# Row tiles of the last expert layer: when the first expert's number is loaded, where the last shared sum is turned, and how the outputs are grouped

## The chip, the cores and the metric

The kernel runs on one core of a Trainium2 chip. The metric is the device time of one execution in microseconds. A core has five engines that run side by side and meet by semaphores: TensorE (PE, matrix products and turns of tiles, results go to PSUM banks), VectorE (DVE), ScalarE (ACT), GpSimd (POOL) and SyncE (SP, which issues transfers). Each executes its own list of instructions in order.

## The reference

Two layers over x, 8 x 256 tokens of 128 features. Each layer is a cross attention and a mixture of experts. The change lies in the last part of the second layer, which computes this:

```python
def _L1_ffn_ref(x_bsD, router_DE, w1_eDF, w3_eDF, w2_eFD, ws1_DF, ws3_DF, ws2_FD):
    B, S, D, E, F, K = (4, 128, 128, 8, 352, 1)
    scores_aE = x_aD @ router_DE
    vals_aK, idx_aK = jax.lax.top_k(scores_aE, K)
    ...
    gates_Ea = jax.nn.sigmoid(masked_aE).T
    routed_in_EaD = jax.lax.stop_gradient(gates_Ea[:, :, None] * x_aD[None, :, :])
    mid_EaF = jax.nn.silu(jnp.einsum('ead,edf->eaf', routed_in_EaD, w1_eDF)) * jnp.einsum('ead,edf->eaf', routed_in_EaD, w3_eDF)
    routed_out_EaD = jnp.einsum('eaf,efd->ead', mid_EaF, w2_eFD)
    shared_aD = jax.nn.silu(x_aD @ ws1_DF) * (x_aD @ ws3_DF) @ ws2_FD
    out_aD = shared_aD + routed_out_EaD.sum(axis=0)
```

Every token goes to one of 8 experts (gate and up matrices of 128 x 352, down matrix of 352 x 128) and to a shared expert of the same shape. The result is x plus both.

## The kernel before

**Shared expert.** The 2048 tokens are taken as 4 blocks of 512. The 352 inner features are cut in three (128, 128, 96), so there are 12 units (`shared_unit`, n = 0 to 11): six products for gate and up on PE, silu on ACT, a multiplication on DVE, and one unit later the down product (`shared_down`) that adds into the bank `SUM`. When a block's three units are done, ACT copies the sum (`copy_sum_1`), PE turns it in four pieces (`finish_1`, L728), and DVE adds it to x (`add_sum_1`, L1460). That sum is called `rest` below: it is what a token has beside its routed expert.

**Sorting.** DVE finds each token's expert and its place in a list that is sorted by expert and cut into tiles of 128 rows. There are 23 row tiles (`TILES`), each of one expert. POOL scatters the gated tokens to `rows_in` in device memory (16 scatters), and x with the shared sum to `rest_in` (16 scatters, `sort_rest`, L1941, four for each block, after that block's add). SP then reads both back in order of tiles, in groups of four tiles (`ROW_GROUPS`): `rows` after all scatters to `rows_in`, `rest_rows` (L2246) after all scatters to `rest_in`.

**Row tiles.** A loop on each engine runs over the tiles j:

- `rows_turn` (PE, L737) turns four tiles' rows at once, ACT and DVE split them into a high and a low part (`split_rows` L1088, `rest_of_rows` L1466). The first group is turned ahead of the loop, the others in the iterations j = 1, 5, 9, 13, 17.
- `gate_up` (PE, L358 to L360, six products) with the expert's matrices, whose address comes from a number: `value_load` (L745) fetches it from `expert_of` into a register of PE.
- `routed_silu` (ACT, L1093), `routed_mul` (DVE, L1473) give `mid`.
- `mid_turn` (PE, L760, three turns), one iteration later, into the bank `SIDE`. `copy_mid` brings the turned tile to SBUF in two parts, ACT (L1098), then DVE (L1489).
- `routed_down` (PE, L772, three products), two iterations later, into the bank `outs` or `misc` by the number of the output group.
- `add_rest` (DVE, L1484) adds `rest_rows` for a whole output group (`OUT_GROUPS`) when its last tile's down product is done. It stands on DVE behind the `routed_mul` and `copy_mid` of the same iteration.
- POOL then scatters the group's tiles to the output, one indirect transfer for each (L1954).

PE's list in iteration j is: products of tile j, turn of the next rows where due, turn of `mid` of tile j-1, down products of tile j-2. The order is written out by hand. A bank is written again only when its last reader is done (`bank_free`); `SIDE` is also the bank of `finish_1`, and `WEIGHT` that of `rows_turn`.

```python
OUT_GROUPS = [range(g, g + 2) for g in range(0, TILES - 3, 2)] + [range(g, g + 1) for g in range(TILES - 3, TILES)]
```

So the tiles go out in ten pairs (0 to 19) and three singles (20, 21, 22).

## Time and profile before

| | us |
|---|---|
| median of 3 runs | 693.57 (693.21 to 693.69) |
| the profiled execution | 696.93 |
| its span, first to last instruction | 695.5 |
| PE busy | 650.4 (94%) |
| DVE busy | 521.2 (75%) |
| POOL busy | 412.1 (59%) |
| ACT busy | 400.8 (58%) |
| row tiles: first product of tile 0 | 640.82 |
| last down product | 691.06 |
| last scatter issued | 693.26 |

The profile is of one execution on the chip; times in it are microseconds from the start of the span. A row of the timeline gives start, duration, engine, line, operation, tiles, count, and in brackets how long the engine had been idle before it and what ended that. "issue" there means that the engine waited for nothing that the profile shows. PE's ends are modelled: its instructions overlap, so the distance of two starts tells more than a duration. The granted clock of PE is at its full level through the row tiles.

### The profile page before, as it was taken

The page shows a single profiled execution, that of the slowest core. Times are in us where ns is not written, and L with a number is a line of the kernel's source. Part 1 is how long each engine was busy: PE and PEld are TensorE (multiplying, and loading weights), DVE is VectorE, ACT ScalarE, POOL GpSimd, SP SyncE. Part 2 cuts the span into 40 slices and gives each one's busy share as a digit, 9 for nine tenths or more (in the row PEclk, how much of TensorE's full clock was granted, in tenths as well). Part 3 has the DMA queues.
Part 4 walks back from the last instruction along what each step waited for, and adds up shares of the span by engine and source line. Part 5 has one row for each costly group of instructions (what it writes and reads, how often), then busy time and mean ns, then how long its engine had stood idle before and what let it go on. Part 6 is the DMA issues. An engine that isn't in the chain of part 4 may idle for free.

```text
span 695.5 us, 14219 instructions
## 1 busy us (share of the span) xinstructions
PE 650.4 (94%) x5301; PEld 343.9 (49%) x5301; DVE 521.2 (75%) x934; ACT 400.8 (58%) x568; POOL 412.1 (59%) x613
## 2 busy tenths in 40 slices
PE   5989999999999999999999999999999999988997
PEld 3333443434343666666656643334434344455897
DVE  4798999999888783942654568898998988766554
ACT  2057777777778634233222257777787777754443
POOL 3444558667412255769954565967977744547445
PEclk9999999999999999999999999999999999999999
DMA  6836635742600576485862406546645545104411
GB/s 175 217 98 163 164 107 126 180 125 60 156 2 3 119 187 139 147 175 144 195 149 78 94 23 149 161 129 153 175 142 120 153 109 177 35 31 133 121 33 39
DMA packets 66601, 84.97 MB, mean 122 GB/s; under 512 B 7776, under 2 KB 48624, under 8 KB 65024
## 3 DMA queue, kind: packets, MB, share of 16 engines
q1 hardware_dynamic: 63856, 79.44, 44.4%
q0 software_dynamic: 1760, 3.62, 1.6%
q10 hardware_dynamic: 916, 1.00, 0.6%
q8 instruction: 43, 0.70, 0.4%
q14 instruction: 26, 0.21, 0.1%
HBM read 57.57 MB, written 25.80 MB: 120 GB/s over the span
## 4 chain that ended last, share of the span: by engine, by line
PE 64%; ACT 12%; DVE 6%; POOL 5%; DMA 5%; issue 4%; SPq 3%; ACTq 0%; DVEq 0%; POOLq 0%
PE pair L497 11%; ACT prob L919 11%; PE misc L510 7%; PE outs L510 6%; PE outs L624 6%; PE pair L458 6%; PE pair L358 5%; PE pair L360 4%; PE pair L359 4%; PE misc L411 3%; DVE negmax L1206 2%; PE outs L396 2%; DMA col<-in_L_b 2%; DMA qstack<-mT 1%; POOL hid L1870 1%
## 5 line engine op out<-in xcount | busy, mean ns | idle before, releaser
L1206 DVE TENSOR_REDUCE negmax<-pair 128x2 f32<-128x1024 f32 x256 | 306.6, 1213 | 37.6 <-PE pair L458 31.6
L919 ACT ACTIVATE prob<-pair 128x1024 f32<-128x1024 f32 x256 | 260.2, 1025 | 89.7 <-PE pair L497 85.3
L497 PE MATMUL pair<-qstack,kstack 54*128 54x256 bf16 x1024 | 100.4, 274 | 20.8 <-ACT prob L919 19.3
L458 PE MATMUL pair<-kstack,qstack 51*128 51x512 bf16 (+1 forms) x512 | 98.1, 379 | 1.6 <-DVE negmax L1206 0.8
L1440 DVE TENSOR_TENSOR hid<-pair,silu 128x512 f32<-128x512 f32 x68 | 46.7, 688 | 70.1 <-PE pair L360 51.3
L497 PEld LDWEIGHTS pair<-qstack,kstack 54*128 54x128 bf16 x1024 | 29.9, 94 | 126.0 <-ACT prob L919 101.1
L1066 ACT ACTIVATE silu<-pair 128x512 f32<-128x512 f32 x68 | 40.6, 599 | 88.6 <-PE pair L360 86.5
L510 PE MATMUL outs<-prob,vaug 128*32 128x256 f32 x1024 | 83.4, 390 | 0.0
L510 PE MATMUL misc<-prob,vaug 128*32 128x256 f32 x1024 | 81.0, 391 | 0.3
L624 PE MATMUL outs<-hid,down 128*128 128x512 f32 x136 | 70.3, 598 | 1.7 <-POOL hid L1870 1.6
L358 PE MATMUL pair<-xT,eh 128*128 128x512 f32 x136 | 70.3, 517 | 0.0
L1870 POOL TENSOR_TENSOR hid<-hid,w_here 128x512 f32<-128x512 f32 x32 | 41.0, 1282 | 40.5 <-DVE hid L1440 40.5
L1792 POOL CAST mparts<-negmax 128x16 bf16<-128x16 f32 x32 | 6.5, 202 | 92.6 <-DVE negmax L1206 92.6
L1870 POOL TENSOR_TENSOR hid<-hid,w_there 128x512 f32<-128x512 f32 x32 | 41.1, 1288 | 26.6 <-DVE hid L1440 26.6
L360 PE MATMUL pair<-xT,e_lo 128*128 128x512 f32 x136 | 53.7, 395 | 0.0
L359 PE MATMUL pair<-xT,eh 128*128 128x512 f32 x136 | 53.2, 391 | 0.0
L1684 POOL TENSOR_SCALAR xn<-x,mv,rstd 128x128 f32<-128x128 f32 x48 | 37.9, 797 | 2.5
L1954 POOL DMA_INDIRECT out_x<-rows,token_of x23 | 22.0, 957 | 25.2 <-DVE rows L1484 20.9
L458 PEld LDWEIGHTS pair<-kstack,qstack 51*128 51x128 bf16 (+1 forms) x512 | 25.3, 94 | 21.9 <-issue 14.6
L1715 POOL TENSOR_TENSOR work<-work,rope 128x512 f32<-128x512 f32 (+1 forms) x32 | 31.4, 1001 | 5.1 <-DMA work<-work 5.0
L358 PEld LDWEIGHTS pair<-xT,eh 128*128 128x128 f32 x136 | 25.6, 188 | 15.2 <-issue 11.7
L510 PEld LDWEIGHTS misc<-prob,vaug 128*32 128x32 f32 x1024 | 20.6, 108 | 24.4 <-issue 11.8
(290 smaller groups left out, 1086.4 us busy)
## 6 DMA issues: line engine op xcount, KB each, us to landing
kstack<-k_terms SPq DMA_DIRECT2D x30, 384.0 KB
w_here<-w_rows SPq DMA_DIRECT2D x32, 256.0 KB, 4.8
w_there<-w_rows SPq DMA_DIRECT2D x32, 256.0 KB, 5.1
k_terms<-kparts SPq DMA_DIRECT2D x16, 384.0 KB, 2.6
qstack<-q_terms SPq DMA_DIRECT2D x30, 192.0 KB, 4.3
ctx_nat<-in_ctxT SPq DMA_DIRECT2D x16, 256.0 KB, 3.2
k_terms<-kparts SPq DMA_DIRECT2D x16, 256.0 KB, 2.9
w_nat<-in_L_gu SPq DMA_DIRECT2D x9, 352.0 KB, 3.7
```

The costliest lines, as they stand in the source:

```text
L358: nc.tensor.matmul(to, w[0], v[0], start=True, stop=False)
L359: nc.tensor.matmul(to, w[0], v[1], start=False, stop=False)
L360: return nc.tensor.matmul(to, w[1], v[0], start=False, stop=True)
L458: return nc.tensor.matmul(to, qstack[n % 3][rows, g, qt * P:(qt + 1) * P], kstack[n % 3][rows, g, :], start=True, stop=True)
L497: e = nc.tensor.matmul(bank[m + r][:, k * SQ:(k + 1) * SQ], kstack[n % 3][rows, g, (c + k) * P:(c + k + 1) * P], qstack[n % 3][rows, g, :] ...
L510: e = nc.tensor.matmul(bank[m][32 * j:32 * j + 32, (quad % 2) * SQ:(quad % 2 + 1) * SQ], vaug[:, KC * (n % 3) + c, h * VC:h * VC + 32], pr ...
L624: nc.tensor.matmul(bank[SUM], down0[:, u, :], hid0[:, m % 4, :], start=place == 0, stop=place == EP).then_inc(d_done, 1)
L919: nc.scalar.activation(prob[:, quad % 2, 2 * g:2 * g + 2, c:c + 2, :].rearrange("p j c q -> p j (c q)"), pair[t_pair(n, step)][:, :, :], A ...
L1066: nc.scalar.activation(silu0[:, m % 2, :], bank[m % 2], ACT.Silu).then_inc(silu_done, 1)
L1206: nc.vector.tensor_reduce(negmax[:, n % 2, 2 * g:2 * g + 2, qt], pair[score_pair(n, step)][:, :, :], AX.X, ALU.max, negate=True).then_inc( ...
L1440: nc.vector.tensor_tensor(hid0[:, m % 4, :], bank[2 + m % 2], silu0[:, m % 2, :], ALU.mult).then_inc(u_mul, 1)
L1870: nc.gpsimd.tensor_tensor(hid0[:, m % 4, :], hid0[:, m % 4, :], weight_buffer(g)[:, w % GROUP, :], ALU.mult).then_inc(w_mul, 1)
```

## The change

Three edits.

1. The number of the first expert is loaded by PE ahead of the first `rows_turn`, not at the head of tile 0.
2. The last block's shared sum (`finish_1(NB - 1)`) is turned behind tile 0's products, not ahead of them. The waits for the weights' low parts stay ahead of tile 0.
3. The output groups are two of four tiles (0 to 3, 4 to 7), five pairs (8 to 17) and five singles (18 to 22). The last tile's `mid` is turned in the bank `WEIGHT`, which no `rows_turn` uses any more then; the two copies read it from there.

```diff
-OUT_GROUPS = [range(g, g + 2) for g in range(0, TILES - 3, 2)] + [range(g, g + 1) for g in range(TILES - 3, TILES)]
+OUT_GROUPS = [range(0, 4), range(4, 8)] + [range(g, g + 2) for g in range(8, TILES - 5, 2)] + [range(g, g + 1) for g in range(TILES - 5, TILES)]
...
+def turning(j):
+
+    return WEIGHT if j == TILES - 1 else SIDE
...
+            def load_expert(j):
+                expert[j] = nc.tensor.value_load(expert_of[0:1, j:j + 1], min_val=0, max_val=E1 - 1)
+
             def gate_up(j):
                 i, k, m = j // 4, j % 4, j % 2
-                expert[j] = e = nc.tensor.value_load(expert_of[0:1, j:j + 1], min_val=0, max_val=E1 - 1)
+                if j > 0:
+                    load_expert(j)
+                e = expert[j]
...
             def mid_turn(j):
                 pe.wait_ge(mid_set, j + 1)
-                bank_free(SIDE)
+                m = turning(j)
+                bank_free(m)
                 for c, (f0, fn) in enumerate(FC):
-                    e = nc.tensor.transpose(bank[SIDE][0:fn, c * P:(c + 1) * P], mid[:, j % 2, f0:f0 + fn], ident[:, :])
+                    e = nc.tensor.transpose(bank[m][0:fn, c * P:(c + 1) * P], mid[:, j % 2, f0:f0 + fn], ident[:, :])
                 e.then_inc(mid_turned, 1)
-                left[SIDE] = midT_b, j + 1
+                left[m] = midT_b, j + 1
...
+                pe.wait_ge(experts_known, 1)
+                load_expert(0)
                 rows_turn(0)
                 shared_down(NB * len(FC) - 1)
-                finish_1(NB - 1)
                 pe.wait_ge(w_low, EP + 1 + len(GU_EARLY))
                 pe.wait_ge(gu_lo, len(GU_LATE))
-                pe.wait_ge(experts_known, 1)
                 for j in range(TILES + 2):
                     if j < TILES:
                         gate_up(j)
+                    if j == 0:
+                        finish_1(NB - 1)
```

The two `copy_mid` (ACT and DVE) read `bank[turning(j)]` instead of `bank[SIDE]`.

PE, from the last unit's down product to tile 0, before. `TENSOR_LOAD expert_of` is the number's load, L728 the turns of the shared sum, L737 those of the rows:

```order
L720 MATMUL outs<-hid,down 128x512 [waits su_mul]
L737 MATMUL pair<-ident,rows 128x128 [waits ld_rows0]
L737 MATMUL pair<-ident,rows 128x128 x3
L720 MATMUL outs<-hid,down 128x512 [waits su_mul]
L728 MATMUL pair<-ident,yT 128x128 [waits ssum_added,ssum_copied]
L728 MATMUL pair<-ident,yT 128x128 x3
L745 TENSOR_LOAD expert_of [waits experts_known,gu_lo,w_low]
L745 ISA x2
L358 ISA [waits ssilu_done,gxT_lo]
L358 MATMUL pair<-gu,gxT 128x352
```

PE, the same place in the changed kernel. The lines are numbered anew: L725 is the down product, L749 the load, L742 the rows, L363 to L365 the products, L733 the shared sum:

```order
L725 MATMUL outs<-hid,down 128x512 [waits su_mul]
L749 TENSOR_LOAD expert_of [waits experts_known]
L749 ISA x2
L742 MATMUL pair<-ident,rows 128x128 [waits ld_rows0]
L742 MATMUL pair<-ident,rows 128x128 x3
L725 MATMUL outs<-hid,down 128x512 [waits su_mul]
L363 ISA [waits gxT_lo,ssilu_done,gu_lo,w_low]
L363 MATMUL pair<-gu,gxT 128x352
...
L365 MATMUL pair<-gu,gxT 128x352
L733 MATMUL pair<-ident,yT 128x128 [waits ssum_added,ssum_copied]
L733 MATMUL pair<-ident,yT 128x128 x3
```

The load has moved from between the shared sum and tile 0 to ahead of the rows; the shared sum's turns have moved from ahead of tile 0's six products to behind them.

DVE, the first add of `rest_rows`, before. It stands ahead of tile 4's multiplication (the first L1473 below it), and holds two tiles (128x2x128):

```order
L1489 COPY hid<-pair 96x128 [waits midT_a]
L1484 TENSOR_TENSOR rows<-outs,rest_rows 128x2x128 [waits rd_done,ld_rest0]
L1473 TENSOR_TENSOR mid<-pair,silu 128x352 [waits mid_turned,rsilu_done,ru_done]
L1489 COPY hid<-pair 96x128 [waits midT_a]
L1473 TENSOR_TENSOR mid<-pair,silu 128x352 [waits mid_turned,rsilu_done,ru_done]
L1466 TENSOR_TENSOR gxT<-pair,gxT 128x512 [waits gxT_hi]
```

DVE in the changed kernel, from tile 4's multiplication on (L1486 is the multiplication, L1479 the split of the rows, L1502 the copy, L1497 the add):

```order
L1486 TENSOR_TENSOR mid<-pair,silu 128x352 [waits mid_turned,rsilu_done,ru_done]
L1502 COPY hid<-pair 96x128 [waits midT_a]
L1486 TENSOR_TENSOR mid<-pair,silu 128x352 [waits mid_turned,rsilu_done,ru_done]
L1479 TENSOR_TENSOR gxT<-pair,gxT 128x512 [waits gxT_hi]
L1480 CAST token_of<-rows 128x4
L1502 COPY hid<-pair 96x128 [waits midT_a]
L1497 TENSOR_TENSOR rows<-outs,rest_rows 128x4x128 [waits rd_done,ld_rest0]
L1486 TENSOR_TENSOR mid<-pair,silu 128x352 [waits mid_turned,rsilu_done,ru_done]
```

The first add has moved behind the multiplications of tiles 4 and 5 and behind the split of the third group of rows, and is of four tiles. On DVE and POOL the end of the list differs by the same table: the adds of tiles 18 and 19 are single there.

## Rows read from the trace of the kernel before

**Rows 1.** The page's first part: busy us, share and count of each engine.

```profile
PE 650.4 (94%) x5301; PEld 343.9 (49%) x5301; DVE 521.2 (75%) x934; ACT 400.8 (58%) x568; POOL 412.1 (59%) x613
```

**Rows 2.** Busy by stretch: length, then PE, PEld, DVE, ACT, POOL, clock, DMA.

```profile
652.00:655.00 3.00, 2.23 (x16) 1.91 (x15) 2.56 (x8) 1.08 (x3) 1.97 (x3) 1.00 1.02 298
...
664.70:689.00 24.30, 24.30 (x185) 23.88 (x186) 12.83 (x34) 10.87 (x26) 11.48 (x13) 1.00 0.11 34
```

**Rows 3.** Timeline of PE from the first rows' turn to tile 1's turn.

```profile
637.45 0.60 PE L737 MATMUL pair<-ident,rows 128*128 128x128 f32 x4
...
639.60 0.66 PE L728 MATMUL pair<-ident,yT 128*128 128x128 f32 x4 [0.69 <-ACT yT L1081]
640.82 0.42 PE L358 MATMUL pair<-gu,gxT 128*128 x1 [0.56 <-issue]
...
642.01 0.42 PE L358 MATMUL pair<-gu,gxT 128*128 x1
...
643.07 0.60 PE L737 MATMUL pair<-ident,rows 128*128 128x128 f32 x4
643.51 0.49 PE L760 MATMUL pair<-ident,mid 128*128 128x128 f32 x3
643.75 0.41 PE L358 MATMUL pair<-gu,gxT 128*128 x1
...
645.44 0.52 PE L760 MATMUL pair<-ident,mid 128*128 128x128 f32 x3 [0.48 <-DVE hid L1489]
```

**Rows 4.** Timeline of DVE at the same place.

```profile
638.72 0.69 DVE L1466 TENSOR_TENSOR gxT<-pair,gxT 128x512 fp32r<-128x512 f32 x1 [1.19 <-ACT gxT L1088]
...
642.16 0.53 DVE L1473 TENSOR_TENSOR mid<-pair,silu 128x352 f32<-128x352 f32 x1 [1.17 <-ACT silu L1093]
```

**Rows 5.** Timeline of DVE, two of the adds of `rest_rows`.

```profile
651.72 0.43 DVE L1484 TENSOR_TENSOR rows<-outs,rest_rows 128x256 f32<-128x256 f32 x1 [2.85 <-DMA rest_rows<-rest_in]
...
663.23 0.41 DVE L1484 TENSOR_TENSOR rows<-misc,rest_rows 128x256 f32<-128x256 f32 x1
```

**Rows 6.** Timeline of PE: tiles 5, 7, 8, 9, 11, and tile 4's turn.

```profile
650.52 0.41 PE L358 MATMUL pair<-gu,gxT 128*128 x1
...
652.91 0.52 PE L760 MATMUL pair<-ident,mid 128*128 128x128 f32 x3 [0.75 <-DVE hid L1489]
...
656.11 0.41 PE L358 MATMUL pair<-gu,gxT 128*128 x1
...
658.07 0.41 PE L358 MATMUL pair<-gu,gxT 128*128 x1
...
660.03 0.41 PE L358 MATMUL pair<-gu,gxT 128*128 x1
...
664.64 0.42 PE L358 MATMUL pair<-gu,gxT 128*128 x1
```

**Rows 7.** Timeline of the end, POOL, DVE and PE.

```profile
688.21 0.96 POOL L1954 DMA_INDIRECT out_x<-rows,token_of  x1 [1.71 <-DVE rows L1484]
...
689.23 0.29 DVE L1489 COPY hid<-pair 96x128 f32<-96x128 f32 x1 [0.15 <-ACT hid L1098]
...
689.48 0.29 DVE L1484 TENSOR_TENSOR rows<-outs,rest_rows 128x128 f32<-128x128 f32 x1
689.66 0.52 PE L760 MATMUL pair<-ident,mid 128*128 128x128 f32 x3 [0.22 <-DVE hid L1489]
...
693.26 0.96 POOL L1954 DMA_INDIRECT out_x<-rows,token_of  x1 [0.30 <-issue]
```

**Rows 8.** DMA issues of the output: count, median us from issue to landing.

```profile
out_x<-rows,token_of POOLq DMA_INDIRECT x23, 2.2
```

**Rows 9.** Timeline of POOL: the first scatter of `rest_in`'s last block.

```profile
642.27 0.96 POOL L1941 DMA_INDIRECT rest_in<-x,row_of  x1 [0.30 <-issue]
```

**Rows 10.** The chain that ended last: the last `rest_in` scatter, the first `rest_rows` transfer.

```profile
646.06 2.23 DMA rest_in<-x,row_of
...
648.30 3.39 DMA rest_rows<-rest_in
```

More of the change, by code:

```diff
@@ L1097, in copy_mid @@
                 act.wait_ge(rd_done, j - 1)
-                nc.scalar.activation(hid1[:, j % 2, 0:2 * P], bank[SIDE][:, 0:2 * P], ACT.Copy).then_inc(midT_a, 1)
+                nc.scalar.activation(hid1[:, j % 2, 0:2 * P], bank[turning(j)][:, 0:2 * P], ACT.Copy).then_inc(midT_a, 1)
             def ffn_1():
@@ L1488, in copy_mid @@
                 ve.wait_ge(midT_a, j + 1)
-                nc.vector.tensor_copy(hid1[0:FC[2][1], j % 2, 2 * P:3 * P], bank[SIDE][0:FC[2][1], 2 * P:3 * P]).then_inc(midT_b, 1)
+                nc.vector.tensor_copy(hid1[0:FC[2][1], j % 2, 2 * P:3 * P], bank[turning(j)][0:FC[2][1], 2 * P:3 * P]).then_inc(midT_b, 1)
             tiles_first, first, end_first, full_first, base, tiles, new, begin, end, shift = (plan[:, i, :] for i in range(10))
```

## The prediction

> **What bounds the kernel now.** I first read the share of each engine: TensorE (PE) is busy 94% of the span, all others below 76% [rows 1]. That share says little about this change, which touches only the last 60 us, so I went on to the busy time by stretch. In the long middle of the row tiles (664.7 to 689.0 us) PE is busy in every microsecond: 24.30 of 24.30 [rows 2]. There a tile costs what its PE work costs, and nothing in the change alters that. What can move is where PE is not full: the step from the shared expert into the first tiles, the place around 652 to 655 us, where PE is busy 2.23 of 3.00 us [rows 2], and what follows PE's last product.
>
> I read these three places in the timeline, engine by engine. "Tile j" is row tile 0 to 22. For each tile PE runs six gate and up products, three turns of `mid` and the down products; in the PE rows the first L358 of a tile is its start.
>
> At the start, PE turns the first rows (637.45), runs the last shared down product, waits for ACT's copy of the sum, turns that at 639.60, and starts tile 0 at 640.82 after 0.56 us in which it waited for nothing that the profile shows [rows 3]. The rows that tile 0 needs were split by DVE at 638.72 + 0.69 = 639.41 [rows 4]. So tile 0 comes 1.41 us after its data.
>
> In the middle, DVE stood still for 2.85 us until 651.72, for the first transfer of `rest_rows` [rows 5]. It was already in the add of tiles 0 and 1, and the multiplications of tiles 4 and 5 were queued behind it. PE waited 0.75 us for that [rows 6].
>
> At the end the chain leaves PE. POOL sends one scatter per tile, 0.96 us plus 0.30 of issue. It sits idle for 1.71 us, starts tile 18 at 688.21 and then runs five back to back until the start of the last at 693.26 [rows 7]. A scatter lands 2.2 us after its issue [rows 8], and that of the last one is the end of the span.
>
> **Part 1: the front.** Two edits. The number of tile 0 is loaded before the rows are turned, and the four turns of the last shared sum go behind tile 0's six products. Cost of a number load on PE: from the sum's turns to tile 0 is 640.82 - 639.60 = 1.22 us; four turns take PE 0.44 us (as at 643.07, after which the next work starts at 643.51) [rows 3]. That leaves 0.78 us for the load and its waits. From tile 0 to tile 1, 1.19 us pass for products that need some 0.97, so there part of the load is hidden. I take 0.7 us.
>
> After the change tile 0 waits only for 639.41. PE starts 0.14 us after a DVE instruction that it waits for (DVE ends at 689.23 + 0.29 = 689.52, PE starts at 689.66 [rows 7]), and a few waits stand before it; I take 639.75. Then tile 0 takes its 1.19 us, as now with tile 1's load in it, and the four turns of the sum add 0.41 to 0.44. Tile 1 starts at about 641.35 instead of 642.01: **0.66 us earlier**. The gain is half of the 1.07 us by which tile 0 moves, because the turns used to lie in front of it and now lie behind.
>
> Does it survive? The turned sum is now ready at about 640.8 + 0.66 = 641.46, so DVE adds it until 642.15, and tile 0's multiplication, queued behind that add, starts at 642.15, where it starts today (642.16 [rows 4]). So tile 0 itself gains nothing. But the next thing that holds PE is the turn of tile 1 at 645.44, behind the second group of rows (turned at 643.07, their split, then DVE's copy) [rows 3]. That chain hangs on the turn of the rows, which comes 0.66 us earlier (2.37 us from 643.07 to 645.44 stay). It gives 644.8, and PE, with tile 2 starting near 643.7 as now, is ready at 644.7. So the 0.66 holds from tile 1's turn on.
>
> The load that stands before the first rows' turn: PE has products in front of it there without a gap, and a load that stands behind a full stretch of products costs nothing between the later tiles (PE is busy throughout [rows 2]). I take 0, since that row is the nearest. Bounds: 0 and 0.78.
>
> The moved turns also feed POOL: the scatters of the last block of `rest_in` wait for this add. They start at 642.27 today, right behind four others [rows 9]. With the add ending at 642.15 they start at about 642.45. Some 0.2 us late, and it must be carried to the next part.
>
> **Part 2: outputs in fours.** The add of tiles 0 to 3 now stands on DVE behind tile 5's multiplication and the third split of rows, not behind tile 3's multiplication. Today's landing is at 648.30 + 3.39 = 651.69 [rows 10]; with the 0.2 it is 651.9. When does DVE get there? Tiles 9 to 11 have the same shape of work without a wait: tile 9 starts at 660.03, the add at 663.23, so 3.20 us later [rows 5, 6]. Tile 5 would start at 650.52 - 0.66 = 649.86, the add at 653.06. That is 1.2 us after the landing: no wait. The stretch from tile 5 to tile 7 takes 656.11 - 650.52 = 5.59 us now, that from 9 to 11 takes 664.64 - 660.03 = 4.61 us [rows 6]. The difference, **0.98 us**, is what the standstill costs PE. An add of four tiles takes 0.69 instead of 0.41 to 0.43 us (0.69 is what the split of 512 columns takes [rows 4], the pairs' adds stand in [rows 5]). The multiplication behind it is 0.1 to 0.3 us later, and PE needs it some 1.3 us after that: covered. The same holds for the add of tiles 4 to 7. POOL gets four scatters at once, 5.0 us of work (4 x 1.26) per 7.8 us of tiles (4 x 1.96, the distance of tile 8 to tile 9 [rows 6]), and has caught up long before the end.
>
> **Part 3: the end.** Tiles 18 and 19 are sent singly. POOL is idle from 686.50, and tile 18's sum is done by then (it comes one tile, some 1.96 us, before tile 19's), so its scatter leaves there and no longer pushes the rest. In today's clock: tile 19 at 688.1; tile 20's add ends at 689.48 + 0.29 = 689.77, its scatter starts at 690.05; then 691.31 and 692.57. Today it is 693.26: **0.69 us**. The last tile's turn goes to another bank, so it need not wait for DVE's copy (PE idle 0.22 by the profile's ends [rows 7]). Worth 0.2 to 0.4 us on PE; it brings the last sum to about 692.2 and so leaves POOL as the bound. Without it the data would be there at 692.6, so that edit alone is worth under 0.1.
>
> **The sum.** 0.66 + 0.98 + 0.69 = 2.33 us. The profiled span of 695.5 us becomes 693.2. The profiled run took 696.93 us, 1.4 more than its span, and 3.4 more than the median of the unprofiled runs (693.57). I take the difference over: 693.57 - 2.33 = **691.24 us**.
>
> **The rivals.**
> *The front gives nothing (20%).* Either the load before the first rows' turn is not hidden (then everything behind is 0.7 later and eats the 0.66), or the 0.56 us was not the load. Result 691.24 + 0.66 = 691.9. For it: no row shows a number load before a turn. Against: the loads between the later tiles cost nothing.
> By the Trainium skill, "Perfetto Trace Analysis", section "Tensor Engine Instruction (MATMUL, LD_WEIGHTS)", a product that waits for a semaphore waits in a queue of the engine while the sequencer goes on to the next instruction. By that rule the load had already run under the wait for the sum, and moving it would bring nothing: 691.9. The trace speaks against it: after the wait, tile 0 still comes 0.78 us later than its four turns allow [rows 3].
>
> *The wait for `rest_rows` stays in some form (12%).* If the transfer lands later than 654.1, four tiles' add holds tile 6's multiplication past PE's need. Then Part 2 gives nothing and the result is 692.2. For it: one group of four now hangs on one wait, and the chain of scatters before it starts 0.2 later. Against: 2.2 us of room.
>
> *Slower (4%).* The same mechanism from a certain point: the last block's scatters to `rest_in` wait for the sum that is now turned later. Each microsecond by which that add is late past 642.15 moves the landing by one. PE stalls from a landing at 654.1 on; the gains are gone at 656.4, and at 657.8, 6.1 us later than today, the kernel is 0.2% slower (695.0). The rows show 0.2 us of that.
>
> *Only the end gains (5%).* 692.9, if both PE gains are met by other waits.
>
> **Numbers.** The forecast has 59%. Differences under 0.2% (1.4 us) can't be told from none here, so "faster" means below 692.2. Faster: nearly all of the first case, most of the second, a third of the third: 0.78. Same 0.18, slower 0.04. Range: below, if PE's tile 0 gains all of its 1.07 us and the rest goes a little better, 690.4; above, the third case, 692.3.
>
> **What would show it.** Right: tile 0 starts near 639.75 and tile 1 near 641.35; DVE's first `rest_rows` add is 128x512, near 653, with no DMA wait; tile 7 at about 654.5 (now 656.11); the last scatter starts near 690.9 in the new span, with short idle times between POOL's last five. Wrong: a gap before the first rows' turn; a DMA wait on DVE; tile 2's turn as late as now; a last scatter that waits for nothing while its data is long there.

## The result

| | before | after |
|---|---|---|
| median of 20 runs, us | 694.75 (691.93 to 697.15) | 693.39 (690.45 to 694.73) |
| ratio, 95% interval | | 0.9972 (0.9960 to 0.9985) |
| profiled execution, its span | 696.93, 695.5 | 693.53, 692.2 |
| measured again, beside 23 runs of before | 695.35 | 692.34 (12 runs), ratio 0.9966 (0.9950 to 0.9982) |

By these ratios the change makes the kernel faster by 1.95 us (1.0 to 2.8), and by 2.36 us in the second comparison. The plain differences of the medians are 1.36 and 3.01 us. The forecast was 2.33 us. The time itself, 693.39, lies 1.1 us above the end of the stated range. On two other chips (whole and whole5 below), on which the kernel before takes 709 to 710 us, the same comparison shows no gain: 0.9991 (0.9968 to 1.0014) and 1.0007 (0.9983 to 1.0031). The experiments come back to them.

Even the executions near 695 us differ by up to 1.8 us in when they reach the row tiles, with the same code up to there but for the number load. I therefore count from the start of the first rows' turn (before 637.45, after 636.56). The profile after, PE's timeline at the start (columns: start, us, engine, line, operation; in brackets the idle time before it and what ended it):

```profile
636.56 0.60 PE L742 MATMUL pair<-ident,rows 128*128 128x128 f32 x4
...
638.87 0.43 PE L363 MATMUL pair<-gu,gxT 128*128 x1 [0.85 <-DVE gxT L1479]
...
639.95 0.60 PE L733 MATMUL pair<-ident,yT 128*128 128x128 f32 x4
640.30 0.41 PE L363 MATMUL pair<-gu,gxT 128*128 x1
...
643.71 0.52 PE L771 MATMUL pair<-ident,mid 128*128 128x128 f32 x3
```

Tile 0 starts 2.31 us after the rows' turn (3.37 in [rows 3]) and now waits for its data, DVE's split. Tile 1 comes at 3.74 instead of 4.56, the turn of its `mid` at 7.15 instead of 7.99.

The same stretch on DVE, and its first `rest_rows` add:

```profile
637.83 0.69 DVE L1479 TENSOR_TENSOR gxT<-pair,gxT 128x512 fp32r<-128x512 f32 x1 [1.19 <-ACT gxT L1101]
...
640.58 0.69 DVE L1473 TENSOR_TENSOR x<-pair,x 128x512 f32<-128x512 f32 x1 [1.99 <-PE pair L733]
...
652.08 0.68 DVE L1497 TENSOR_TENSOR rows<-outs,rest_rows 128x512 f32<-128x512 f32 x1
```

The wait of 2.85 us [rows 5] is gone; the add now takes four tiles at once. PE, tiles 5, 7, 9 and 11 in turn:

```profile
648.89 0.41 PE L363 MATMUL pair<-gu,gxT 128*128 x1
...
653.44 0.42 PE L363 MATMUL pair<-gu,gxT 128*128 x1
...
657.37 0.41 PE L363 MATMUL pair<-gu,gxT 128*128 x1
...
661.98 0.43 PE L363 MATMUL pair<-gu,gxT 128*128 x1
```

Tile 5 to tile 7 takes 4.55 us (5.59 in [rows 6]), about the same as tile 9 to 11 (4.61). By stretch (length, then busy us of PE, PEld, DVE, ACT, POOL, granted clock, DMA share, GB/s) the hole that stood there is filled, and the long stretch stays full:

```profile
652.00:655.00 3.00, 3.00 (x24) 2.81 (x23) 1.70 (x5) 1.31 (x3) 1.67 (x2) 1.00 1.01 291
664.70:689.00 24.30, 24.20 (x185) 23.27 (x183) 12.85 (x35) 10.58 (x25) 14.00 (x16) 1.00 0.13 41
```

The end, on POOL and DVE:

```profile
685.47 0.95 POOL L1967 DMA_INDIRECT out_x<-rows,token_of  x1 [0.31 <-DVE rows L1497]
687.44 0.96 POOL L1967 DMA_INDIRECT out_x<-rows,token_of  x1 [1.02 <-DVE rows L1497]
688.70 0.96 POOL L1967 DMA_INDIRECT out_x<-rows,token_of  x1 [0.30 <-issue]
689.96 0.95 POOL L1967 DMA_INDIRECT out_x<-rows,token_of  x1 [0.30 <-issue]
...
689.01 0.29 DVE L1497 TENSOR_TENSOR rows<-misc,rest_rows 128x128 f32<-128x128 f32 x1 [0.71 <-PE misc L783]
```

The backlog of five scatters [rows 7] has shrunk to three, and the last starts 0.66 us after its data.

### The profile page after: what moved, and what is told of

It is laid out like the page before. It is cut to its first block, busy times and chain, and to the rows that moved or that the text cites. A ratio compares the mean times of both kernels' runs of the same rounds, so it can differ in the third digit from the quotient of the medians.

```text
span 692.2 us, 14218 instructions
## 1 busy us (share of the span) xinstructions
PE 650.1 (94%) x5301; PEld 344.3 (50%) x5301; DVE 521.0 (75%) x933; ACT 400.4 (58%) x568; POOL 412.0 (60%) x613
## 4 chain that ended last, share of the span: by engine, by line
PE 69%; ACT 12%; DVE 6%; DMA 4%; POOL 3%; issue 3%; SPq 2%; ACTq 0%; DVEq 0%; POOLq 0%
PE pair L502 11%; ACT prob L932 11%; PE misc L515 7%; PE outs L629 7%; PE outs L515 6%; PE pair L363 6%; PE pair L463 6%; PE pair L365 5%; PE pair L364 5%; PE misc L416 3%; DVE negmax L1219 2%; PE outs L401 2%; DMA col<-in_L_b 2%; DMA qstack<-mT 1%; PE outs L725 1%
## 5 line engine op out<-in xcount | busy, mean ns | idle before, releaser
L363 PE MATMUL pair<-xT,eh 128*128 128x512 f32 x136 | 70.3, 517 | 0.0
L365 PE MATMUL pair<-xT,e_lo 128*128 128x512 f32 x136 | 53.7, 395 | 0.0
L363 PEld LDWEIGHTS pair<-xT,eh 128*128 128x128 f32 x136 | 25.6, 188 | 15.1 <-issue 11.7
```

The source lines that it names most:

```text
L363: nc.tensor.matmul(to, w[0], v[0], start=True, stop=False)
L365: return nc.tensor.matmul(to, w[1], v[0], start=False, stop=True)
```

## Experiments

Marks of the runs, in us behind each kernel's first rows' turn ("front" is the number load ahead and the sum's turn behind the first products):

| kernel | tile 0 | tile 1 | tile 5 | tile 7 | tile 22 | last scatter |
|---|---|---|---|---|---|---|
| before | 3.37 | 4.56 | 13.07 | 18.66 | 49.78 | 55.81 |
| after | 2.31 | 3.74 | 12.33 | 16.88 | 48.06 | 53.40 |
| whole6 (after again) | 2.31 | 3.74 | 12.37 | 16.92 | 48.12 | 53.45 |
| e_nofours | 2.31 | 3.74 | 12.39 | 20.64 | 51.80 | 57.15 |
| e_front2 | 2.31 | 3.72 | 16.54 | 21.37 | 53.03 | 59.26 |
| e_front3 | 2.36 | 4.04 | 17.64 | 22.19 | 53.71 | 59.89 |
| whole5 (after again) | 2.38 | 4.07 | 16.47 | 21.02 | 57.84 | 63.54 |
| e_fours4 | 4.54 | 5.73 | 19.59 | 24.18 | 59.36 | 65.55 |
| e_end2 | 4.39 | 6.31 | 19.69 | 24.42 | 55.99 | 61.68 |

The first four rows are from chips on which the kernel before takes about 695 us, the others from chips on which it takes 708 to 710. What differs there is told below; up to some 590 us both kinds of run agree to within 5 us. The kernel before was timed there but not traced; e_end2, which differs from it only at the end of the list, stands in for it. A *stop* below is a time in which an engine stands still although the profile shows its inputs there.

### First set: each part of the front, and the fours

**e_front**: front alone (`turning(j)` is always `SIDE`, `OUT_GROUPS` as before).

> The two edits at the front alone (number of tile 0 loaded ahead of the first rows' turn, last shared sum turned behind tile 0); output groups and the last turn as before. All times here are counted from the start of the first rows' turn on PE, since the stages ahead differ by some tenths of a us from run to run. Before: tile 0 at 3.37, tile 1 at 4.56, tile 7 at 18.66, last scatter at 55.81. Whole change: 2.31, 3.74, 16.88, 53.40. Theory (parts add up): tile 0 at 2.3, tile 1 at 3.7 (0.8 earlier than before). DVE still stands still at the first add of rest_rows, and since the landing of that transfer doesn't move (or moves 0.2 later), PE's gain of 0.8 is lost in a longer wait there: tile 7 at 18.7 to 18.9, last scatter at 55.8 to 56.0, no gain at all. Rival (the sum as I forecast it, each part on its own): tile 7 at 17.9 and the last scatter at 55.0.

704.83 us, a single time, beside 708.14 of before. Tile 0 comes at 3.12 and not at 2.3, because the rows' split on ACT and DVE is late in this run. As in before, DVE's first add waits for the transfer:

```profile
658.07 0.43 DVE L1497 TENSOR_TENSOR rows<-outs,rest_rows 128x256 f32<-128x256 f32 x1 [2.58 <-DMA rest_rows<-rest_in]
```

**e_load**: the number load ahead, the sum's turn where it was.

```diff
+                pe.wait_ge(experts_known, 1)
+                load_expert(0)
                 rows_turn(0)
```

> Only the number of tile 0 is loaded ahead; the last shared sum is turned ahead of tile 0, as before. Counted from the first rows' turn (before: shared sum's turns at 2.15, tile 0 at 3.37). Theory: the 1.22 us from the shared sum's turns to tile 0 shrink to the 0.44 that four turns take and some tenths for waits, tile 0 at 2.6 to 2.8; the first rows' turn comes no later behind the down product ahead of it (0.85 us after it, as before). Rival (a waiting product doesn't hold up the load behind it, the 0.56 us were something else): tile 0 stays at 3.3 to 3.4. Rival (load not hidden): rows' turn 0.7 later behind the down product.

PE from the rows' turn to tile 0:

```profile
642.26 0.60 PE L742 MATMUL pair<-ident,rows 128*128 128x128 f32 x4
...
645.43 0.66 PE L733 MATMUL pair<-ident,yT 128*128 128x128 f32 x4 [0.69 <-ACT yT L1093]
645.84 0.41 PE L363 MATMUL pair<-gu,gxT 128*128 x1
```

From the sum's turn to tile 0 it is 0.41 us; in [rows 3] it is 1.22, and in the six other traced kernels that keep the load there (e_fours to e_fours4, e_end, e_end2) it is 1.19 to 1.29. So the number load cost PE 0.81 us, although it stands behind an instruction that waited 0.69 us for ACT. The time of the whole run (707.52) says nothing here: tile 3 comes 7.8 us after tile 2 (2.4 in the changed kernel).

**e_sumbehind**: the turn behind, the load where it was (in `gate_up`).

```diff
-                finish_1(NB - 1)
                 pe.wait_ge(experts_known, 1)
 ...
                     gate_up(j)
+                    if j == 0:
+                        finish_1(NB - 1)
```

> Only the last shared sum is turned behind tile 0; the number of tile 0 is loaded at its head, as before. Counted from the first rows' turn. Theory: the number load has the time until the rows' split at 1.96 (the last down product and the wait for the split) to run in, so tile 0 comes at 2.3, as in the whole change, and tile 1 at 3.7: then the load ahead brings nothing once the sum is out of the way. Rival: the load stands behind the wait for the last down product's input and is exposed, tile 0 at 2.9 to 3.0.

707.91 us. Tile 0 at 2.58, tile 1 at 4.00. PE around it:

```profile
646.44 1.12 PE L725 MATMUL outs<-hid,down 96*128 96x512 f32 x2 [0.80 <-DVE hid L1466]
647.62 0.43 PE L363 MATMUL pair<-gu,gxT 128*128 x1
```

The last shared down product waited 0.80 us for a late multiplication on DVE, and tile 0 follows it directly. So the 0.27 us by which tile 0 is later than in the changed kernel is no price of the load. The turn behind alone brings at least 0.79 of tile 0's 1.06 us, and the load alone took 0.81 from the same stretch: the two edits are not a sum. Whether the load ahead still brings something once the turn is out of the way is not shown.

**e_fours**: `OUT_GROUPS` with two groups of four, three singles, nothing else.

> Only the first two output groups are of four tiles; front and end as before. Counted from the first rows' turn (before: tile 5 at 13.07, tile 7 at 18.66, last scatter at 55.81). Theory: DVE's first add of rest_rows waits for no transfer, or for under 0.3 us, tile 5 to tile 7 takes 4.6 instead of 5.6, tile 7 at 17.7, last scatter at 54.8 (1.0 earlier). Rival (the wait for rest_rows only moves to the add of four): tile 7 stays at 18.4 to 18.7.

716.67 us, a single time, with stops of many microseconds in the row tiles. Inconclusive; e_fours2 to e_fours4 repeat it.

### Second set: the parts with intervals

**whole** is the changed kernel, **e_front2** and **e_fours2** repeat the above, **e_end** has five singles at the end and pairs before:

```diff
-OUT_GROUPS = [range(g, g + 2) for g in range(0, TILES - 3, 2)] + [range(g, g + 1) for g in range(TILES - 3, TILES)]
+OUT_GROUPS = [range(g, g + 2) for g in range(0, TILES - 5, 2)] + [range(g, g + 1) for g in range(TILES - 5, TILES)]
```

> The whole change once more, as the yardstick of this set. Theory: 1.4 to 2.8 us faster than the kernel before on the same chip (2.0 by the comparison so far). In the profile, counted from the first rows' turn on PE (before: tile 0 at 3.37, tile 1 at 4.56, tile 7 at 18.66, last scatter at 55.81): 2.31, 3.74, 16.88, 53.40, to within 0.3. Rival (the differences of single runs are as large as the change, and the profile of the first comparison was a lucky one): other intervals by over 0.5, with engines idle for something that isn't in the program.

> The two edits at the front alone, once more (in the first run of it engines stood still for microseconds while all their inputs were there, so that its intervals can't be read). Theory: tile 0 at 2.3, tile 1 at 3.7 after the first rows' turn, but the first add of rest_rows waits longer for its transfer (3.5 us instead of 2.85) and tile 7 stays at 18.7 to 18.9, last scatter at 55.8 to 56.0: no gain, 0 to 0.2 us slower. Rival (as I summed it up): tile 7 at 17.9, last scatter at 55.0, 0.7 faster.

> The two groups of four alone, once more. Theory: tile 5 to tile 7 takes 4.6 instead of 5.6, tile 7 at 17.7, last scatter at 54.8, 1.0 us faster than before. Rival (the wait for rest_rows only moves to the add of four): tile 7 at 18.4 to 18.7.

> Only the end: tiles 18 and 19 single, last tile turned in the other bank; the first groups are pairs and the front is as before. Theory: tile 7 at 18.7 as before, last scatter 0.65 to 0.7 earlier, at 55.1; 0.7 us faster. Rival (PE, not POOL, bounds the end once tiles 18 and 19 are single): the last scatter waits for the last add, 55.3 to 55.5.

| | us | ratio, 95% |
|---|---|---|
| whole | 709.43 | 0.9991 (0.9968 to 1.0014) |
| e_front2 | 708.18 | 0.9961 (0.9940 to 0.9981) |
| e_fours2 | 712.70 | 1.0034 (1.0010 to 1.0057) |
| e_end | 710.25 | 0.9992 (0.9974 to 1.0011) |

Against the expectations, the front alone was the best and the fours alone lost.

The traces show one half of the reason: on these chips the wait that the fours remove is mostly not there. Stops in tiles 1 to 5 bring DVE to its first `rest_rows` add after the transfer has landed. With pairs that add waited for the transfer in e_front alone (2.58 us); in e_load, e_sumbehind, e_front2, e_front3, e_end and e_end2 it stood idle for 0.03 to 0.65 us, and not for the transfer. Tile 5 to tile 7 takes 4.55 to 4.85 us in these six, against 4.55 to 4.63 in whole, whole5 and e_fours2 to e_fours4. So there was little for the fours to gain, and no wait for the transfer that could take the front's gain back. What the fours lost is told with the fourth set.

From tile 22 to the last scatter e_end takes 5.76 us (6.23 in e_front2, whose end is that of before), about the gain that was expected for it.

### Third set: the price of a load, a late landing, another place for the add

**e_loads3** leaves two more loads of the same number beside the first (useless work). **e_late4** delays the last block of `rest_in` by four additions on POOL (useless work too). **e_next** moves the last shared sum to behind tile 1's products and the turn of tile 0's `mid` (into the bank `misc`) and the adds of the fours one iteration later.

```diff
 load_expert(0)
+load_expert(0)
+load_expert(0)
```
```diff
+for i in range(4 if blk == NB - 1 else 0):
+    nc.gpsimd.tensor_tensor(wnat[:, :, :], wnat[:, :, :], wnat[:, :, :], ALU.add).then_inc(filled, 1)
+    pool.wait_ge(filled, i + 1)
```
```diff
-                    if j == 0:
+                    if j == 1:
                         finish_1(NB - 1)
...
+                        if j == g[-1] + (3 if len(g) == 4 else 2):
+                            add_rest(i)
```

> The whole change, but the number of tile 0 is loaded three times ahead of the first rows' turn (the first two loads have no use). In the whole change the first rows' turn starts 0.86 us after the first pass of the down product ahead of it, 0.85 without the load: one load there costs nothing. Theory (PE's instructions run ahead of its products there, by more than one load): with two more loads the turn comes 0.7 to 1.6 us later, since two more can't all be hidden, and tile 0 still 2.3 after the turn. Rival (the loads never hold up products): 0.86 stays. Each load's price can be read from it. Where the chip holds engines up by itself (they stand still with all inputs there, at the same places in all kernels of a chip), only distances without such a stop are compared.

> The whole change, with four additions on GpSimd (384 columns each, of no use) ahead of the last block's scatters to rest_in; about 1.3 us each, so the landing of rest_rows is some 5 us later. Theory: from a landing 2.2 us later than in the whole change on, PE pays each further microsecond: tile 5 to tile 7 takes 4.55 + 2.5 to 3 us, DVE waits 3.5 to 4 us for the transfer at the add of four tiles, and the kernel is 0.3 to 1 us slower than before. Rival (PE has more room, since tile 6's multiplication is all that hangs on it): tile 5 to 7 stays under 5.5.

> The whole change, and the last shared sum goes further back: turned behind tile 0's turn into the bank misc, which nobody uses then, and added on DVE behind the second split of rows; in return the adds of four tiles stand one tile later on DVE. Theory: the second rows' turn comes 0.4 earlier, at 4.4 instead of 4.8 after the first, and since the chain to tile 1's turn hangs on it, tiles 3 and later are 0.2 to 0.4 earlier than in the whole change; the transfer of rest_rows lands 2.7 later, which the later add just covers (no stop at tile 7). 0.3 us faster than the whole change, which the timing can't tell. Rival (the later landing comes back as a wait): tile 7 and later as in the whole change or later, with a DMA wait on DVE.

> The two groups of four alone, a third time. In the second run they were 0.34% slower than before on their chip, on which engines stopped for microseconds with all their inputs there, at the same places in every kernel. Theory (on a chip without these stops the effect is the one I summed up): tile 5 to tile 7 4.6 instead of 5.6, 1.0 us faster. Rival (the groups of four themselves cost, e.g. by the scatters that go out late and at once): 0.2 to 0.5% slower again, and the profile shows it behind tile 7, where POOL's scatters or DVE hold PE.

e_loads3, 714.79 us, one run, PE:

```profile
648.09 1.02 PE L725 MATMUL outs<-hid,down 128*128 128x512 f32 x2
649.30 0.65 PE L742 MATMUL pair<-ident,rows 128*128 128x128 f32 x4 [0.20 <-issue]
```

The rows' turn comes 1.21 us behind the down product; after it is 0.86 (636.56 behind 635.70), and 0.85 before. So one load is hidden there and of three 0.35 us shows, in one run; I had expected 0.7 to 1.6 us more.

e_late4, 704.83 us, one run: POOL and DVE:

```profile
646.73 3.55 POOL L1965 TENSOR_TENSOR wnat<-wnat 128x384 f32<-128x384 f32 x4
...
654.36 0.96 POOL L1956 DMA_INDIRECT rest_in<-x,row_of  x1 [0.30 <-issue]
```
```profile
659.64 0.69 DVE L1499 TENSOR_TENSOR rows<-outs,rest_rows 128x512 f32<-128x512 f32 x1 [1.19 <-DMA rest_rows<-rest_in]
```

With the block 3.8 us later the group of four does wait, for 1.19 us, so the room is finite. The price that I expected (a wait of 3.5 to 4 us, 2.5 to 3 us more from tile 5 to tile 7) did not come. That stretch takes 5.42 us instead of 4.55, which is the rival's figure, and its extra time lies ahead of the add, where ACT stood still for 2.10 us; tile 6 to tile 7, behind the add, takes 1.99. When PE begins to pay for a late landing is not shown. e_next gained nothing (710.89 us, ratio 1.0013, 0.9993 to 1.0033), and e_fours3 lost again (710.85 us, 1.0033, 1.0013 to 1.0053).

### Fourth set: the parts once more

> The whole change again, on another chip. By the theory that the three parts gain what the two undisturbed profiles show (0.84 us at tile 1's turn, about 0.9 more by tile 7, 0.63 at the end, 2.41 in all), the ratio is 0.9965 where engines do not stop with their inputs there; first tile 2.3 us and last scatter some 53.4 us behind the first rows' turn. By the rival that the gain of the two long profiles was one of level between runs, the ratio is 1.000. Where stops of microseconds lie in the row tiles again, the ratio is unclear and the marks up to the first stop are what counts.

> The kernel before with its first eight output tiles in two groups of four, nothing else. By the theory that the grouping takes away the wait of rest_rows' first add (2.85 us) without a price, it is 0.7 to 1.1 us faster than before (ratio 0.9985 to 0.999) where engines do not stop. By the rival that the grouping has a price of its own, which the two runs on stopping chips (1.0034 and 1.0033) showed, it is slower by some 2.3 us again, and the rows of tiles 0 to 8 show where.

> The kernel before with its last five output tiles scattered one by one instead of three. Theory: last scatter 0.6 us earlier (ratio 0.999); last add's data ready 0.3 us ahead of the last scatter's start. Rival: the two added scatters cost their 1.26 us apart each and nothing is gained, 1.000 to 1.002.

> The kernel before with the first expert's number loaded ahead and the last shared sum's turn behind the first gate products. Theory: tile 0 at 2.3 and tile 1's turn at 7.1 us behind the first rows' turn (before 3.37 and 7.99), of which 0 to 0.8 us reach the end, since the wait of the first rest_rows add (2.85 us before) takes the rest back: that add waits longer by what the tiles are earlier, ratio 0.999 to 1.000. Rival: nothing takes it back and the ratio is that of the 10 runs earlier, 0.996 (2.8 us).

| | us | ratio, 95% |
|---|---|---|
| whole5 | 709.71 | 1.0007 (0.9983 to 1.0031) |
| e_fours4 | 712.69 | 1.0059 (1.0027 to 1.0090) |
| e_end2 | 709.78 | 1.0006 (0.9991 to 1.0021) |
| e_front3 | 707.14 | 0.9972 (0.9945 to 0.9999) |

The same order again, again on a chip with stops. In e_fours4 one of them stands at tile 13. A scatter on POOL and the copy on ACT there:

```profile
682.39 0.96 POOL L1954 DMA_INDIRECT out_x<-rows,token_of  x1 [0.30 <-issue]
684.63 0.39 ACT L1098 ACTIVATE hid<-pair 128x256 f32<-128x256 f32 x1 [2.37 <-remote]
```

Tile 9 to 10 takes 3.26 us and tile 13 to 14 5.80 in it; in the traced kernels whose first groups are pairs both take 2.40 to 2.42. From tile 9 to tile 16 the seven kernels with pairs take 15.2 to 15.6 us on these chips (15.1 in the trace of before, which has no stops). Eight kernels with the fours take 16.7 to 20.6 us, and e_next 23.0. So every kernel with the fours has stops there, of 1 to 8 us in all, that the pairs don't have.

They go with something that the rows do show. In each of these nine kernels POOL sends four scatters back to back and then four or six more (in e_fours4 at 667.29 to 672.05 and at 676.07 to 683.35), and in each a stop begins inside or at the end of such a run. The pairs send at most two at a time there. In e_next, whose adds of four stand an iteration later, the stops begin at tiles 10 and 14 and not 9 and 13. That is where they lie, not a cause: on the chips without stops the changed kernel sends the same four and six back to back, and nothing stops. What makes engines stop is not shown.

### Fifth set: the change without its fours

```diff
-OUT_GROUPS = [range(0, 4), range(4, 8)] + [range(g, g + 2) for g in range(8, TILES - 5, 2)] + ...
+OUT_GROUPS = [range(g, g + 2) for g in range(0, TILES - 5, 2)] + ...
```

> The changed kernel with its first eight tiles back in groups of two: front and end of the change without the fours. Theory for a chip on which engines stop with their inputs there: the grouping in fours costs what extra stops take around tiles 9 to 15 (each kernel that has it showed intervals of 3.3 to 6.4 us there, none without it did), so this one keeps the front's gain: ratio 0.996 to 0.997 (2 to 3 us) and even intervals of tiles 9 to 15. Rival: the fours gain their 0.9 us and the others' sum is what it is on an undisturbed chip: ratio 0.998, worse than the whole change. On a chip without such stops both theories give 0.9978 to 0.9985 for it and the DMA wait of the first rest_rows add grows to 3.6 us.

> The whole change beside the one without fours, on the same chip. By the theory of a place-dependent price of the fours: ratio 0.999 to 1.001 on a stopping chip, 2 us behind the kernel without them. By the rival: 0.9965 to 0.9975, 0.9 us ahead of it. On a chip without stops: 0.9965 and ahead of it by the wait that the fours take away.

This set ran on a chip without stops. e_nofours took 696.36 us, ratio 1.0013 (0.9992 to 1.0033); whole6 692.34 us, ratio 0.9966 (0.9965 expected). My figure for such a chip, 0.9978 to 0.9985, was wrong: without the fours the other two parts together show no gain. The wait of the first add, expected at 3.6 us, was 4.05. DVE and PE of e_nofours at tiles 4 to 6:

```profile
650.42 0.43 DVE L1497 TENSOR_TENSOR rows<-outs,rest_rows 128x256 f32<-128x256 f32 x1 [4.05 <-DMA rest_rows<-rest_in]
```
```profile
651.61 0.52 PE L771 MATMUL pair<-ident,mid 128*128 128x128 f32 x3 [1.95 <-DVE hid L1502]
```

The front brings DVE to the add earlier, the transfer does not land earlier, so the wait grows from 2.85 to 4.05 us and PE's idle time from 0.75 [rows 6] to 1.95. Then comes something that before did not have. By stretch, e_nofours (the column after POOL's is the granted clock):

```profile
651.00:652.00 1.00, 0.39 (x4) 0.42 (x5) 1.00 (x4) 0.00 (x0) 0.88 (x1) 1.00 1.08 321
652.00:653.00 1.00, 1.00 (x9) 0.87 (x8) 1.00 (x4) 0.38 (x1) 0.69 (x2) 0.82 1.10 310
653.00:654.00 1.00, 1.00 (x4) 1.00 (x5) 0.28 (x1) 0.00 (x0) 0.69 (x2) 0.50 0.62 189
654.00:655.00 1.00, 1.00 (x5) 0.93 (x5) 0.09 (x1) 0.46 (x1) 0.69 (x2) 0.50 0.08 25
655.00:656.00 1.00, 1.00 (x7) 0.99 (x6) 0.47 (x2) 0.38 (x1) 0.87 (x1) 0.50 0.20 66
656.00:657.00 1.00, 1.00 (x9) 1.00 (x9) 0.25 (x1) 0.00 (x0) 0.00 (x0) 0.97 0.20 66
```

After the idle time TensorE ran for more than 3 us at a granted clock of 0.50, which is 1.2 of its 2.4 GHz: 4 to 5 products in a microsecond instead of 9 to 10. Tile 6 to 7 took 3.51 us instead of 1.99. From tile 5 to 7 that makes 8.25 us, 3.70 more than with the fours (4.55). DVE in whole6, for comparison, has no such wait:

```profile
651.93 0.68 DVE L1497 TENSOR_TENSOR rows<-outs,rest_rows 128x512 f32<-128x512 f32 x1
```

The clock also orders the single runs. Of e_nofours' 12, four have a mean clock of 0.997 or more, with a median of 693.89 us; the other eight 697.61. Of before's 23 beside them, 12 have it (694.66), 11 don't (695.68). In whole6 it is 8 (692.07) and 4 (693.20).

So the loss is not in every execution. In the four at the higher clock the kernel without its fours is 0.77 us faster than before at that clock, about what the end alone gives (0.69): there the longer wait takes back the front and no more. In the eight others the clock costs on top. That is a reading of four and eight runs, and only one of them was traced.

## Why the prediction was right in its steps and missed in its time

**The front, 0.66: right, 0.82 measured.** Tile 0 comes 1.06 us earlier, as forecast (1.07). For tile 0 to tile 1 with the turns between them I had 1.60 us, and it took 1.43: the turns take 0.35 there, and tile 0's products up to them 1.08 instead of 1.19, so tile 1's load seems better hidden. From tile 1's turn on 0.84 remains, as the "does it survive" step had it. The load ahead of the rows' turn costs nothing (0.86 against 0.85); e_loads3 shows where that ends. The rival that the front gives nothing falls for the whole change, on the chips without stops. In the Trainium skill, "Perfetto Trace Analysis", section "Tensor Engine Instruction (MATMUL, LD_WEIGHTS)", the sequencer goes on while a product waits. By that rule the load in the kernel before would have been hidden already; the trace of e_load does not agree, since tile 0 moved by 0.81 us against the sum's turn.

**The middle, 0.98: right, 1.04 measured (5.59 to 4.55).** The last block's first scatter came 4.99 us behind the rows' turn; forecast 5.00. DVE reached the add at 15.52; forecast 15.61. What I had as a fixed number is the room. I put the landing at 14.45 and the room at 1.2 us. With the last block's scatters at the same marks, the transfer was issued and landed at 11.03 and 14.77 in e_nofours, at 12.34 and 15.04 in after and at 11.01 and 14.08 in whole6. DVE's add came 0.48 us behind the landing in after and 1.49 in whole6. It was enough in both, in after by little. Why the transfer was issued 1.3 us later there is not shown.

What the step did not say is how much hangs on it. It priced the fours against the kernel before. Beside the front they are worth 3.76 us at tile 7 in the traced executions (20.64 without them, 16.88 with them). From tile 5 to tile 7 that is 1.04 for the old wait, 1.20 by which the front makes PE's idle time longer (1.95 for 0.75), and some 1.5 for the clock (3.51 us for 1.99 from tile 6 to 7), which not every execution pays.

So the three terms do not add up part by part, and the sum came out right only because all three were in it: 0.66 + 0.69 without 0.98 would have been 1.35 faster, and measured is no gain (1.0013). The same error stands in the rival whose "wait for `rest_rows` stays": it was priced at 692.2, with the front's 0.66 kept.

**The end, 0.69: right.** From tile 22's start to the last scatter it is 6.03 us before and 5.34 after (48.06 to 53.40), 0.69 less. On the chips with stops it is 6.18 (e_front3) and 5.69 (e_end2), 0.49 less. The end alone was not run on a chip without stops; where it was, its ratios (0.9992 and 1.0006) can't be told from 1. The last scatter now starts 0.66 us after its data; I had 0.37 (692.2 to 692.57). POOL is the bound at the end, as forecast, with 0.3 us more room than I gave it.

**The sum.** Tile 7 comes 1.78 us earlier (forecast 1.64), the last scatter 2.41 (forecast 2.33). The three parts measured add up to 2.55; some 0.1 us is lost again between tiles 1 and 5 and between tiles 7 and 22. That it lands within 0.1 of the forecast is in part luck. The ratios say 1.95 and 2.36 us.

**The failed step is the last line of the sum**: "693.57 - 2.33". It took the median of three runs that lay within 0.5 us of each other as the level to subtract from. Twenty runs of the same kernel spread from 691.93 to 697.15, with a median of 694.75, 1.18 above the three. The median after lies 2.15 us above the forecast, 1.18 of it by the level and 0.97 because the medians differ by 1.36 and not by 2.33. My range had room for the second and none for the first: without the level's 1.18, 693.39 would have been 692.2, just inside. Part of the spread is the clock: of the 20 runs after, the six with a mean clock of 0.999 or 1.000 have a median of 691.71 us, the eight at 0.994 to 0.996 one of 694.11. The row that warned of it was there: the profiled execution took 3.4 us more than the median of the three, and I carried that difference over as if it belonged to profiling.

**What stays open** is why the fours lose on chips with stops. The rows put the loss into stops at tiles 9 to 16, inside or behind runs of four to six scatters, but don't tell what causes them. The kernel without fours was to test it there and ran on a chip without stops. Nor were the front alone, the fours alone or the end alone run on a chip without stops: what each would give there alone is read from the traces of the kernels that have them together.

## What to carry to other kernels

Price a wait at the length that it has after the other parts of the same change: work that is shortened ahead of a late transfer only lengthens the wait, and can cost TensorE its clock on top, so move the consumer of the transfer first. Three runs that agree say little of where twenty will lie: forecast the difference, and give the range the spread of the level. Time a part on the kind of chip on which the whole was timed; a wait that one chip has can be missing on another.

## What the runs showed of the hardware

- A number load into a register of PE cost it 0.81 us where products wait on it (e_load), even though the instruction ahead of it waits 0.69 us for another engine. Ahead of the first rows' turn, behind a filled stretch, one cost nothing (0.86 against 0.85 us) and three 0.35 us (e_loads3, one run).
- In e_nofours, after 1.95 us without a product, TensorE ran for more than 3 us at half its clock (0.50). After the 0.75 us of the kernel before it did not (1.00 in [rows 2]). The length of the idle time alone does not decide it. Ahead of the row tiles both kernels have the same one of 1.77 us, before (first) and e_nofours (second):

```profile
611.58 1.12 PE L720 MATMUL outs<-hid,down 128*128 128x512 f32 x2 [1.77 <-DVE hid L1455]
608.10 1.94 PE L725 MATMUL outs<-hid,down 128*128 128x512 f32 x2 [1.77 <-DVE hid L1468]
```

The three microseconds that hold these rows, again before first:

```profile
611.00:614.00 3.00, 2.42 (x10) 1.67 (x11) 1.54 (x3) 0.72 (x2) 1.57 (x2) 1.00 0.14 47
608.00:611.00 3.00, 2.90 (x6) 1.67 (x7) 0.65 (x3) 0.38 (x1) 1.09 (x2) 0.55 0.14 47
```

The same code kept its clock in one execution and lost it in the other.

- Chips differ. In the first comparison and in the last set the kernel before takes about 695 us, on the four chips of the other sets 708 to 710. On these, engines stand still for microseconds from about 600 us on, in every kernel traced there. In e_fours4 the first long one is at a transpose on DVE and a silu on ACT:

```profile
609.55 0.72 DVE L1213 STREAM_TRANSPOSE o_found<-misc 128x512 f32<-128x512 f32 x1 [8.35 <-remote]
609.66 0.60 ACT L1077 ACTIVATE silu<-pair 128x512 f32<-128x512 f32 x1 [4.86 <-remote]
```

PE had nothing to do meanwhile (0.01 us busy from 606 to 609), and its granted clock fell to half:

```profile
609.00:612.00 3.00, 0.35 (x1) 0.35 (x2) 2.35 (x5) 0.60 (x1) 0.00 (x0) 0.51 0.00 0
612.00:615.00 3.00, 3.00 (x10) 2.52 (x10) 1.33 (x6) 0.60 (x1) 0.61 (x2) 0.50 0.00 0
```

On such chips a gain of 2 us can be hidden or undone by where the stops fall, and only distances in the trace that hold no stop are of use.
